# A state-space scan in eight chunks: a ring of eight units, one C product for two units, and the layer norm before it moved into the expert stage

## The chip, the cores and the metric

The kernel runs on one core of a Trainium2 chip. The core has a matrix engine (TensorE, here PE, with its weight loads PEld), three vector engines (VectorE or DVE, ScalarE or ACT, GpSimd or POOL) and SyncE (SP), which here only issues DMAs. Each engine works through its own queue strictly in the order written; the engines meet through semaphores. The metric is the time of one execution on the device in microseconds (us), lower is better.

## The reference, cut to what matters

Two layers of a transformer with adaptive layer norm work on 2048 tokens of 512 features. Layer 0 is a softmax attention and a layer of eight experts (each token goes to one). Layer 1 is a selective state space and an MLP on permuted features. The change touches the end of layer 0 and the state space:

```python
x = x + gb * experts(h)                       # layer 0's end
h = layernorm(x) * (1 + ca) + sa              # the norm before the state space
proj = h @ W_in.T; u, gate = split(proj, 2)   # 1024 channels each
u = silu(causal_conv4(u) + conv_b)
dt, B, C = split(u @ Wx.T, [32, 48])          # each RMS-normalised; B and C have 16 states
delta = softplus(dt @ Wdt.T + dt_bias)
state = exp(delta * A) * state + (delta * u) * B     # for each token, channel and state
y = (state * C).sum(states) + u * D
x = x + ga * ((y * silu(gate)) @ W_out.T)
```

## The kernel before, in words

The program is a row of stages (`qkv`, `attention`, `experts`, `state_space`, `permuted_mlp`), each with its own block of five instruction streams; a stage begins when the one before has ended on all engines. Between stages the activations lie in device memory.

**The end of `experts`.** Tokens are sorted by expert, multiplied tile by tile (23 tiles, L922), scaled on DVE (L1085) and stored. Then POOL gathers the results of the 16 token tiles back (L848), DVE adds each to x (L1089), PE turns it so that features lie on partitions (L931), ACT copies it out (L972) and SP stores it to `x_layer0`, features by tokens (L818).

**The state space.** The 2048 tokens go in 8 chunks of 256 (`SCH`, `SW`), the 1024 channels in 8 tiles of 128 (`DT`). The scan works in units: one unit is four of a tile's 16 states for 128 channels, laid out as 128 partitions (32 channels by 4 states) times 4 groups of channels (`J`) times 256 tokens. A tile has 4 units (`GROUPS`), a chunk 32 (`UNITS`), the whole run 256. For unit q of chunk c:
- SP has stored delta and delta*u of the tile and loaded them back repeated on all state partitions (`repeat`, L1246 to L1256, two slots), and B and C rows as well (`bc_rows`).
- ACT writes the decays exp(delta*A) into PSUM, two instructions of 256 for each half bank, three half banks in all (`decays`, L1636). It waits until the scans that use a half bank have read it.
- The input (delta*u)*B of 1024 elements a partition is written into a place of the ring `scan`, by POOL for even units (L1328) and by DVE for odd ones (L1745, `spread`). The ring has `RING = 4` places; a place is free when PE has summed the unit that used it.
- DVE scans: four instructions of 256 tokens (L1760); after an odd unit it carries the last states over (L1765).
- POOL multiplies the unit by C in place (L1343), one instruction of 1024 elements.
- PE sums over states (L1467, eight instructions), and after the fourth unit adds u*D (L1472). DVE gates the tile into `y` (`gate_y`, L1774), at the unit after next but one: at q = 2 mod 4 it gates the tile before.

All other work of the stage is woven in at fixed units. The table `AT` gives for each unit q of a chunk the product that PE does before it sums unit q: projections, convolution, gates and rows of the next chunk, the layer norm's products of the chunk after that, the output of the chunk before. They share two PSUM banks; each waits until the product two places earlier has been read. `U_COPY`, `CONV_OUT`, `GATE_OUT`, `STEP_OUT` and others give the unit before whose decays ACT reads them; `CENTRED`, `NORM`, `RESIDUAL`, `DELTA` and others the same for DVE. Before the scan, `FIRST` lists chunk 0's products and the layer norm of chunk 1. The layer norm with features on partitions takes a mean and a variance product on PE, a centring (L1700) and a scaling (L1706) of 1024 elements on DVE and squares on ACT. The output (L1457) is multiplied by the gate ga and added to x on DVE (`residual`, L1780).

## Time and profile before

| | us |
|---|---|
| median of 3 runs | 1993.42 |
| lowest, highest | 1985.92, 1998.05 |
| profiled execution, its own time | 1997.48 |
| span of its trace | 1995.7 |

The page of the profile, busy time and share of the span: PE 1644.5 us (82%), PEld 881.9 (44%), DVE 1394.3 (70%), ACT 1083.1 (54%), POOL 998.4 (50%). The mean granted clock of TensorE is 0.818 of full speed. In 40 equal slices, each digit the busy share in tenths:

```profile
PE   6888999999689994869689697896978969755758
PEld 2522232232256443747356474663746637422422
DVE  3258888886173112048999989899899898999523
ACT  2334666667511112265857668576685766754227
POOL 0000000001054004138898888888888888999413
PEclk8766999999855995869588696896978969766778
DMA  5311000000292436233443444434444344544122
```

One slice is 49.9 us. The stages: the attention fills slices 4 to 11, the experts 11 to 16, the state space runs from 784.65 us to about 1897 us (slices 16 to 38), the MLP takes the rest. A row for a group reads: line, engine, operation, written<-read by the program's names, shapes, xcount, then busy us and mean ns of one, then the engine's idle time before it and what released it. PEclk is the clock that the throttle granted, 1.0 being 2.4 GHz and 0.5 being 1.2 GHz.

### The profile page before, as it was taken

To read this page: it belongs to the slowest core of one execution; us is meant where nothing else is said; L and a number is where in the kernel's file an instruction comes from. 1 tells how busy PE (TensorE), PEld (TensorE's weight loads), DVE (VectorE), ACT (ScalarE), POOL (GpSimd) and SP (SyncE) were. 2 spreads that over 40 slices of the span, in tenths; PEclk is the share of its full clock that TensorE was granted. 3 is DMA by queue.
4 is the path that set the end of the run, shared out by engine and by line. 5 is a ranking of instruction groups with operands and counts; after the bars stand their busy time and mean duration, and the time that the engine had idled before them with its cause. 6 is when DMAs were issued, how large, how long until landed. Compare 5 with 4: busy or idle time off the path is not lost. (4 is left out here: it accounts for less than half of the span.)

```text
span 1995.7 us, 24404 instructions
## 1 busy us (share of the span) xinstructions
PE 1644.5 (82%) x8256; PEld 881.9 (44%) x8256; DVE 1394.3 (70%) x2276; ACT 1083.1 (54%) x1989; POOL 998.4 (50%) x590
## 2 busy tenths in 40 slices
PE   6888999999689994869689697896978969755758
PEld 2522232232256443747356474663746637422422
DVE  3258888886173112048999989899899898999523
ACT  2334666667511112265857668576685766754227
POOL 0000000001054004138898888888888888999413
PEclk8766999999855995869588696896978969766778
DMA  5311000000292436233443444434444344544122
GB/s 220 150 55 50 3 3 3 3 3 4 40 354 98 132 111 231 95 89 92 112 101 85 109 119 108 111 80 106 112 114 117 82 102 106 120 102 98 35 100 85
DMA packets 150747, 191.58 MB, mean 96 GB/s; under 512 B 17715, under 2 KB 122947, under 8 KB 148958
## 3 DMA queue, kind: packets, MB, share of 16 engines
q1 hardware_dynamic: 142508, 167.19, 30.9%
...
q8 instruction: 66, 1.08, 0.2%
q14 instruction: 57, 0.47, 0.1%
...
## 5 line engine op out<-in xcount | busy, mean ns | idle before, releaser
L1760 DVE TENSOR_TENSOR_SCAN ssm_scan<-ssm_psum,ssm_state,ssm_scan 128x256 f32<-128x256 f32 x1024 | 678.7, 728 | 49.8 <-ACT ssm_psum L1636 49.3
L1343 POOL TENSOR_TENSOR ssm_scan<-ssm_scan,ssm_bc 128x1024 f32<-128x1024 f32 x256 | 553.5, 2175 | 60.0 <-DVE ssm_scan L1760 58.8
L1636 ACT ACTIVATE ssm_psum<-ssm_rep,ssm_a 128x256 f32<-128x256 f32 x1024 | 433.4, 468 | 168.4 <-DVE ssm_scan L1760 167.9
L1467 PE MATMUL ssm_psum<-ssm_scan,ssm_select 128*32 128x256 f32 x2048 | 204.7, 481 | 199.3 <-POOL ssm_scan L1343 199.2
L1328 POOL TENSOR_TENSOR ssm_scan<-ssm_rep,ssm_bc 128x1024 f32<-128x1024 f32 x128 | 301.1, 2353 | 62.8 <-PE ssm_psum L1467 53.1
L640 ACT ACTIVATE att_probs<-att_psum 128x1024 f32<-128x1024 f32 x256 | 248.3, 1021 | 104.5 <-PE att_psum L576 104.2
L677 DVE TENSOR_REDUCE att_rowmax<-att_psum 128x1 f32<-128x512 f32 x448 | 277.9, 682 | 38.0 <-PE att_psum L558 38.0
L1467 PEld LDWEIGHTS ssm_psum<-ssm_scan,ssm_select 128*32 128x32 f32 x2048 | 45.8, 119 | 316.4 <-POOL ssm_scan L1343 216.4
L529 POOL COPY att_v<-v_tokens 128x128 f32<-128x128 f32 x8 | 2.3, 292 | 328.0 <-ACT att_out L634 328.0
L558 PE MATMUL att_psum<-att_k,att_q 72*128 72x512 bf16 x448 | 159.3, 395 | 3.7 <-DVE att_rowmax L677 2.2
L1745 DVE TENSOR_TENSOR ssm_scan<-ssm_rep,ssm_psum 128x1024 f32<-128x1024 f32 x128 | 155.5, 1215 | 8.5 <-PE ssm_psum L1467 5.8
L1408 PE MATMUL ssm_psum<-ssm_h,ssm_win 128*128 128x256 f32 x512 | 133.0, 419 | 9.6 <-DMA ssm_win<-in_win 6.1
L587 PE MATMUL att_psum<-att_probs,att_v 128*32 128x512 f32 x1024 | 137.2, 608 | 0.6 <-ACT att_probs L640 0.6
L576 PE MATMUL att_psum<-att_q,att_k 74*128 74x512 bf16 x448 | 132.2, 379 | 0.7 <-ACT att_probs L640 0.2
L1457 PE MATMUL ssm_psum<-ssm_y,ssm_wout 128*128 128x256 f32 x512 | 131.9, 417 | 0.6 <-DVE ssm_y L1774 0.6
L1408 PEld LDWEIGHTS ssm_psum<-ssm_h,ssm_win 128*128 128x128 f32 x512 | 108.1, 214 | 33.6 <-issue 15.9
L1416 PE MATMUL ssm_psum<-ssm_upre,ssm_conv 128*128 128x256 f32 x512 | 120.3, 388 | 0.0
L1457 PEld LDWEIGHTS ssm_psum<-ssm_y,ssm_wout 128*128 128x128 f32 x512 | 107.0, 212 | 26.7 <-issue 5.0
L1450 PE MATMUL ssm_psum<-ssm_h,ssm_win 128*128 128x256 f32 x512 | 118.0, 384 | 0.1
L1416 PEld LDWEIGHTS ssm_psum<-ssm_upre,ssm_conv 128*128 128x128 f32 x512 | 95.7, 191 | 24.4 <-issue 11.6
L1450 PEld LDWEIGHTS ssm_psum<-ssm_h,ssm_win 128*128 128x128 f32 x512 | 95.4, 190 | 21.3 <-issue 9.0
L558 PEld LDWEIGHTS att_psum<-att_k,att_q 72*128 72x128 bf16 x448 | 35.1, 98 | 132.0 <-DVE att_rowmax L677 96.1
...
## 6 DMA issues: line engine op xcount, KB each, us to landing
ssm_rep<-drive_rows SPq DMA_DIRECT2D x256, 256.0 KB, 4.4
...
```

The lines of the kernel that those rows point to most:

```text
L558: nc.tensor.matmul(ps_m[n % MB], q[0:QROWS, tile[m // QC]], k[0:QROWS, chunk[m % QC]], start=True, stop=True).then_inc(max_scored, 1)
L640: nc.scalar.activation(probs[:, u % RING, :].rearrange("p (j t) -> p j t", j=2), ps_s[u % 2], ACT.Exp).then_inc(exp_done, 1)
L677: nc.vector.tensor_reduce(rowmax[:, m:m + 1], ps_m[n % MB], AX.X, ALU.max).then_inc(max_done, 1)
L1328: nc.gpsimd.tensor_tensor(drive[:, Q % RING], rep[:, s % 2, 1], bc[:, c % 2, 0, gr, :].unsqueeze(1).to_broadcast([P, J, SW]), ALU.mult).th ...
L1343: nc.gpsimd.tensor_tensor(read[:, Q % RING], drive[:, Q % RING], bc[:, c % 2, 1, gr, :].unsqueeze(1).to_broadcast([P, J, SW]), ALU.mult).t ...
L1408: last = nc.tensor.matmul(halves("proj", c, pair)[:, i], win[:, k, m:m + P], h[:, k, :], start=(k == 0), stop=(k == KT - 1))
L1416: last = nc.tensor.matmul(halves("conv", c, pair)[:, i], conv[:, 2 * pair + i, k, :], upre[:, pair % 2, i, k:k + SW], start=(k == 0), stop ...
L1450: last = nc.tensor.matmul(halves("gate", c, pair)[:, i], win[:, k, m:m + P], h[:, k, :], start=(k == 0), stop=(k == KT - 1))
L1457: last = nc.tensor.matmul(bank("out", c, m)[:, 0:SW], wout[:, t, m * P:(m + 1) * P], y[:, c % 2, t, :], start=(t == 0), stop=(t == DT - 1))
L1467: last = nc.tensor.matmul(ps_y[t % 2][32 * j:32 * j + 32, :], select[:], read[:, Q % RING, j, :], start=(gr == 0), stop=False)
L1636: nc.scalar.activation(ps_decay[n % HALF_BANKS][:, i], rep[:, s % 2, 0, j, :], ACT.Exp, scale=amat[:, t, gr, j:j + 1]).then_inc(decay_done, 1)
L1760: nc.vector.tensor_tensor_scan(drive[:, Q % RING, j, :], ps_decay[(2 * Q + j // 2) % HALF_BANKS][:, j % 2], drive[:, Q % RING, j, :], stat ...
```

## The change

- **Ring.** `RING` goes from 4 to 8 places. To make room the weights of the state space lie in the buffer that held the expert weights, u in a buffer shared with the experts' tail, and `y` is gone: the gated output overwrites its gate. So a new gate may be copied only after the output product that reads the old one; the outputs move from units 16, 17, 27, 28 to 10, 11, 12, 14, the gate products from 10, 11, 12, 14 to 16, 17, 27, 28, and the gate's SiLU from unit 20 to 31.
- **C product.** POOL issues one product of 2048 elements after each odd unit, for it and the even unit before, and its own input for even units three units ahead instead of two.
- **Layer norm.** It is computed in the tail of `experts`, with tokens on partitions: DVE adds, takes statistics, normalises every fourth tile; ACT takes square roots and normalises the others; PE turns the normalised rows, ACT copies them, SP stores x (tokens by features) and the normalised rows (features by tokens). The state space only modulates them. The input half of `W_in` is loaded on ACT's queue in that tail.
- **Output.** `W_out` is multiplied by ga once on POOL; x is added by PE, as products of x's rows against the identity into the same bank (two per output); ACT copies the result out.
- **Chunk 0.** Two of its gate products, two of its step products and the gate's SiLU move behind the start of the scan (units 0 to 5).

```diff
+            pe.wait_ge(y_done, TILES)
             for t in range(TT):
-                pe.wait_ge(x2_done, t + 1)
-                if t >= len(ps_x2):
-                    pe.wait_ge(x2_out, t - len(ps_x2) + 1)
+                pe.wait_ge(*normalised(t))
+                if t >= len(ps_hn):
+                    pe.wait_ge(hn_out, t - len(ps_hn) + 1)
                 for k in range(KT):
-                    last = nc.tensor.transpose(ps_x2[t % len(ps_x2)][:, k * P:(k + 1) * P], x[:, t, k * P:(k + 1) * P], g.ident[:])
-                last.then_inc(x2_mm, 1)
+                    last = nc.tensor.transpose(ps_hn[t % len(ps_hn)][:, k * P:(k + 1) * P], back[:, t, k * P:(k + 1) * P], g.ident[:])
+                last.then_inc(hn_mm, 1)
...
+            act.wait_ge(y_mm, TILES)
+            wsrc = d["win"].rearrange("(k p) m -> p k m", p=P)
+            act.dma_start(win[:, :, 0:DI], wsrc[:, :, 0:DI]).then_inc(g.win_in[0], 16)
+
+            def deviation2(t):
+                act.wait_ge(var2_done, t + 1)
+                nc.scalar.activation(sd[:, t:t + 1], meanvar[:, t, 1:2], ACT.Sqrt, bias=g.ln_eps[:, 0:1]).then_inc(sd2_done, 1)
+
+            def normalise2(t):
+                act.wait_ge(shift2_done, on_act(t) + 1)
+                nc.scalar.activation(back[:, t], x[:, t], ACT.Identity, bias=shift2[:, t:t + 1], scale=rstd[:, t:t + 1]).then_inc(hn_act, 1)
+
+            def turn_out(t):
+                c, at = t // TC, t % TC * P
+                act.wait_ge(hn_mm, t + 1)
+                if c >= TSLOTS and t % TC == 0:
+                    act.wait_ge(g.hn_stored[c % TSLOTS], 16 * (c // TSLOTS))
+                nc.scalar.copy(hnt[:, c % TSLOTS, :, at:at + P], ps_hn[t % len(ps_hn)].rearrange("p (k t) -> p k t", k=KT)).then_inc(hn_out, 1)
+
+            for n in range(TT + 4):
+                if 0 <= n - 1 < TT:
+                    deviation2(n - 1)
+                if 0 <= n - 2 < TT and n - 2 not in DVE_NORMS:
+                    normalise2(n - 2)
+                if n - 4 >= 0:
+                    turn_out(n - 4)
...
+            for n in range(TT + 2):
+                if 0 <= n - 2 < TT:
+                    inverse2(n - 2)
+                if n < TT:
+                    add(n)
+                if 0 <= n - 1 < TT:
+                    variance2(n - 1)
+                if 0 <= n - 2 < TT:
+                    normalise2(n - 2)
+                if n < TT:
+                    statistics2(n)
...
-    RING = 4
+    RING = 8
...
-        AT = {0: ("proj", 0), 1: ("proj", 1), 3: ("conv", 0), 4: ("proj", 2), 5: ("conv", 1), 6: ("proj", 3), 7: ("conv", 2), 8: ("mean", 0),
-              9: ("conv", 3), 10: ("gate", 0), 11: ("gate", 1), 12: ("gate", 2), 13: ("rows", 0), 14: ("gate", 3), 15: ("square", 0),
-              16: ("out", 0), 17: ("out", 1), 18: ("var", 0), 19: ("rms", 0), 20: ("bcast", 0), 21: ("step", 0), 22: ("step", 1),
-              24: ("step", 2), 25: ("step", 3), 27: ("out", 2), 28: ("out", 3)}
-        AHEAD = {"proj": 1, "conv": 1, "gate": 1, "rows": 1, "square": 1, "rms": 1, "step": 1, "mean": 2, "var": 2, "bcast": 2, "out": -1}
-        FIRST = (("mean", 0, 0), ("var", 0, 0), ("bcast", 0, 0), ("proj", 0, 0), ("proj", 0, 1), ("conv", 0, 0), ("proj", 0, 2), ("conv", 0, 1),
-                 ("proj", 0, 3), ("conv", 0, 2), ("conv", 0, 3), ("gate", 0, 0), ("gate", 0, 1), ("rows", 0, 0), ("gate", 0, 2), ("square", 0, 0),
-                 ("gate", 0, 3), ("rms", 0, 0), ("step", 0, 0), ("step", 0, 1), ("step", 0, 2), ("step", 0, 3),
-                 ("mean", 1, 0), ("var", 1, 0), ("bcast", 1, 0))
+        AT = {0: ("proj", 0), 1: ("proj", 1), 3: ("conv", 0), 4: ("proj", 2), 5: ("conv", 1), 6: ("proj", 3), 7: ("conv", 2),
+              9: ("conv", 3), 10: ("out", 0), 11: ("out", 1), 12: ("out", 2), 13: ("rows", 0), 14: ("out", 3), 15: ("square", 0),
+              16: ("gate", 0), 17: ("gate", 1), 19: ("rms", 0), 21: ("step", 0), 22: ("step", 1),
+              24: ("step", 2), 25: ("step", 3), 27: ("gate", 2), 28: ("gate", 3)}
+        AHEAD = {"proj": 1, "conv": 1, "gate": 1, "rows": 1, "square": 1, "rms": 1, "step": 1, "out": -1}
+        FIRST = (("proj", 0, 0), ("proj", 0, 1), ("conv", 0, 0), ("proj", 0, 2), ("conv", 0, 1), ("proj", 0, 3), ("conv", 0, 2), ("conv", 0, 3),
+                 ("rows", 0, 0), ("square", 0, 0), ("rms", 0, 0), ("step", 0, 0), ("gate", 0, 0), ("gate", 0, 1), ("step", 0, 1))
+        LATE = {0: ("gate", 2), 1: ("step", 2), 2: ("gate", 3), 3: ("step", 3)}
...
-        U_COPY, CONV_OUT, GATE_OUT = {3: 0, 4: 1, 7: 2, 9: 3}, {6: 0, 8: 1, 10: 2, 12: 3}, {13: 0, 14: 1, 15: 2, 17: 3}
-        SILU, ROWS_OUT, RMS, SQUARE, GATE_SILU, RSTD, H_OUT = 13, 16, 18, 19, 20, 21, 24
+        U_COPY, CONV_OUT, GATE_OUT = {3: 0, 4: 1, 7: 2, 9: 3}, {6: 0, 8: 1, 10: 2, 12: 3}, {18: 0, 19: 1, 29: 2, 30: 3}
+        SILU, ROWS_OUT, RMS, GATE_SILU, H_OUT = 13, 16, 18, 31, 24
+        LATE_GATE, LATE_STEP, LATE_SILU, LATE_DELTA = {2: 2, 4: 3}, {3: 2, 5: 3}, 5, {3: 2, 5: 3}
...
-        CENTRED, NORMED, NORM = 11, 21, 22
+        NORMED = 21
         DELTA = {24: 0, 25: 1, 27: 2, 28: 3}
-        RESIDUAL = {19: 0, 20: 1, 30: 2, 31: 3}
+        OUT_COPY = {12: 0, 13: 1, 14: 2, 16: 3}
...
+            pool.wait_ge(g.win_in[2], 16)
+            pool.wait_ge(row_out, 1)
+            for t in range(DT):
+                nc.gpsimd.tensor_tensor(wout[:, t], wout[:, t], gate_row, ALU.mult).then_inc(wout_gated, 1)
+
             drive_input(0, 0)
             drive_input(0, 1)
-            for Q in range(2):
+            for Q in range(4):
                 if not ON_DVE[Q]:
                     spread(Q)
             for c in range(SCH):
                 for q in range(UNITS):
                     t, gr = q // GROUPS, q % GROUPS
                     Q = c * UNITS + q
-                    if Q + 2 < SCH * UNITS and not ON_DVE[(q + 2) % UNITS]:
-                        spread(Q + 2)
-                    pool.wait_ge(scan_done, (Q + 1) * J)
-                    nc.gpsimd.tensor_tensor(read[:, Q % RING], drive[:, Q % RING],
-                                            bc[:, c % 2, 1, gr, :].unsqueeze(1).to_broadcast([P, J, SW]), ALU.mult).then_inc(read_done, 1)
+                    if gr % 2:
+                        if Q + 3 < SCH * UNITS:
+                            spread(Q + 3)
+                        pool.wait_ge(scan_done, (Q + 1) * J)
+                        pair = slice((Q - 1) % RING, Q % RING + 1)
+                        nc.gpsimd.tensor_tensor(read[:, pair], drive[:, pair],
+                                                bc[:, c % 2, 1, gr - 1:gr + 1, :].unsqueeze(2).to_broadcast([P, 2, J, SW]), ALU.mult).then_inc(read_done, 2)
...
             def output(c, m):
                 if m == 0:
                     pe.wait_ge(ygate_done, (c + 1) * DT)
+                    pe.wait_ge(wout_gated, DT)
                 for t in range(DT):
-                    last = nc.tensor.matmul(bank("out", c, m)[:, 0:SW], wout[:, t, m * P:(m + 1) * P], y[:, c % 2, t, :], start=(t == 0), stop=(t == DT - 1))
+                    nc.tensor.matmul(bank("out", c, m)[:, 0:SW], wout[:, t, m * P:(m + 1) * P], gate[:, c % 2, t, :], start=(t == 0), stop=False)
+                if m == 0:
+                    pe.wait_ge(xres_in, 16 * (c + 1))
+                for s in range(ST):
+                    last = nc.tensor.matmul(bank("out", c, m)[:, s * P:(s + 1) * P], xres[:, s, m * P:(m + 1) * P], g.ident[:], start=False, stop=(s == ST - 1))
                 last.then_inc(out_mm, 1)
...
-                    act.wait_ge(ygate_done, (c - 1) * DT)
+                    act.wait_ge(out_mm, (c - 1) * KT)
...
+            def copy_out(c, m):
+                act.wait_ge(out_mm, c * KT + m + 1)
+                if m == 0:
+                    act.wait_ge(wout_gated, DT)
+                    if c >= 1:
+                        act.wait_ge(x3_stored, 16 * c)
+                nc.scalar.copy(xout[:, m, :], bank("out", c, m)[:, 0:SW]).then_inc(x3_done, 1)
...
+            modulate(1)
+            copy_rows(0)
+            inverse_rms(0)
+            step_out(0, 0)
             copy_gate(0, 0)
             copy_gate(0, 1)
-            copy_rows(0)
-            copy_gate(0, 2)
-            inverse_rms(0)
-            copy_gate(0, 3)
-            for pair in range(DP):
-                step_out(0, pair)
-            silu_gate(0)
-            norm_chunk(1)
+            step_out(0, 1)
...
-                nc.vector.tensor_tensor(y[:, c % 2, t, :], ps_y[t % 2], gate[:, c % 2, t, :], ALU.mult).then_inc(ygate_done, 1)
-
-            def residual(c, m):
-                if m == 0:
-                    dve.wait_ge(xres_in, 16 * (c + 1))
-                dve.wait_ge(out_mm, c * KT + m + 1)
-                nc.vector.scalar_tensor_tensor(xres[:, m, :], bank("out", c, m)[:, 0:SW], gates[:, m:m + 1], xres[:, m, :],
-                                               ALU.mult, ALU.add).then_inc(x3_done, 1)
...
```

On SP's queue the load of a chunk's rows now waits for that chunk's buffer (two instead of one), `store(c - 1)` stands before the fifth tile of chunk c instead of `store(c - 2)` before the first, and the rows of x for the output are loaded before tile 1 instead of tile 2.

## Rows read from the trace of the kernel before

**Rows 1.** Busy time by stretch: PE, PEld, DVE, ACT, POOL, then clock, DMA.
```profile
1257.74:1383.00 125.26, 106.71 (x596) 70.63 (x596) 113.70 (x186) 84.47 (x188) 110.52 (x56) 0.84 0.44 104
...
1757.00:1872.00 115.00, 57.27 (x344) 24.70 (x344) 109.97 (x175) 55.05 (x126) 110.20 (x55) 0.61 0.37 91
```

**Rows 2.** Waits from 1257 to 1383 us: total, times, longest.
```profile
ACT ssm_upre L1548 <- PE ssm_psum L1408: 11.3, 4, 5.2
...
DVE ssm_scan L1760 <- ACT ssm_psum L1636: 7.5, 6, 2.6
```

**Rows 3.** Timeline of DVE (start, us, instruction): last carry of chunks 0 and 6.
```profile
1007.75 0.17 DVE L1765 TENSOR_REDUCE ssm_state<-ssm_scan 128x8 f32<-128x8 f32 x1
...
1758.59 0.17 DVE L1765 TENSOR_REDUCE ssm_state<-ssm_scan 128x8 f32<-128x8 f32 x1
```

**Rows 4.** Groups by line and shape: busy us, mean ns, idle before.
```profile
L1343 POOL TENSOR_TENSOR ssm_scan<-ssm_scan,ssm_bc 128x1024 f32<-128x1024 f32 x256 | 553.5, 2175 | 60.0 <-DVE ssm_scan L1760 58.8
...
L1328 POOL TENSOR_TENSOR ssm_scan<-ssm_rep,ssm_bc 128x1024 f32<-128x1024 f32 x128 | 301.1, 2353 | 62.8 <-PE ssm_psum L1467 53.1 <-DMA ssm_rep<-drive_rows 9.6
...
L1316 POOL TENSOR_TENSOR ssm_du<-ssm_delta,ssm_u 128x256 f32<-128x256 f32 x64 | 46.6, 728 | 54.5 <-DVE ssm_delta L1734 54.5
...
L1700 DVE TENSOR_TENSOR ssm_x<-ssm_x,ssm_psum 128x1024 f32<-128x1024 f32 x8 | 9.6, 1201 | 20.0 <-PE ssm_psum L1384 20.0
...
L1780 DVE SCALAR_TENSOR_TENSOR ssm_xres<-ssm_psum,mod,ssm_xres 128x256 f32<-128x256 f32 x32 | 15.0, 470 | 17.6 <-PE ssm_psum L1457 17.6
...
L1001 DVE BATCH_NORM_STATS2 moe_stat<-moe_x 128x6 f32<-128x512 f32 x16 | 11.0, 685 | 0.0
```

**Rows 5.** Timelines of POOL, PE and ACT around the same stretch.
```profile
1256.99 4.30 POOL L1343 TENSOR_TENSOR ssm_scan<-ssm_scan,ssm_bc 128x1024 f32<-128x1024 f32 x2
...
1261.35 1.08 PE L1467 MATMUL ssm_psum<-ssm_scan,ssm_select 128*32 128x256 f32 x8 [1.05 <-POOL ssm_scan L1343]
...
1263.38 5.66 PE L1408 MATMUL ssm_psum<-ssm_h,ssm_win 128*128 128x256 f32 x16
...
1269.53 3.72 PE L1408 MATMUL ssm_psum<-ssm_h,ssm_win 128*128 128x256 f32 x16
...
1273.18 0.64 PE L1467 MATMUL ssm_psum<-ssm_scan,ssm_select 128*32 128x256 f32 x8
...
1269.07 0.59 ACT L1548 COPY ssm_upre<-ssm_psum 128x512 f32<-128x512 f32 x1 [5.15 <-PE ssm_psum L1408]
...
1269.55 1.67 ACT L1636 ACTIVATE ssm_psum<-ssm_rep,ssm_a 128x256 f32<-128x256 f32 x4
```

**Rows 6.** Timeline of PE: four single matmul instructions against the identity.
```profile
1215.36 1.06 PE L1398 MATMUL ssm_psum<-ident,ssm_rstd 128*128 128x128 f32 x4
```

**Rows 7.** Timeline of DVE at the start of chunk 3.
```profile
1257.85 1.22 DVE L1745 TENSOR_TENSOR ssm_scan<-ssm_rep,ssm_psum 128x1024 f32<-128x1024 f32 x1
...
1258.99 2.67 DVE L1760 TENSOR_TENSOR_SCAN ssm_scan<-ssm_psum,ssm_state,ssm_scan 128x256 f32<-128x256 f32 x4
...
1264.54 0.42 DVE L1774 TENSOR_TENSOR ssm_y<-ssm_psum,ssm_gate 128x256 f32<-128x256 f32 x1
```

**Rows 8.** Groups by line: SiLU and the table loads around it.
```profile
L1561 ACT ACTIVATE ssm_u<-ssm_u 128x2048 f32<-128x2048 f32 x8 | 15.3, 1910 | 0.1
...
L1518 ACT ACT_TABLE_LOAD x17 | 21.8, 1283 | 4.9 <-PEq L716 4.6
```

**Rows 9.** Timeline of ACT: starts of two successive step outputs, chunk 0.
```profile
857.03 0.84 ACT L1597 ACTIVATE ssm_delta<-ssm_psum,ssm_dtb 128x256 f32<-128x256 f32 x2 [1.75 <-PE ssm_psum L1443]
...
859.86 0.83 ACT L1597 ACTIVATE ssm_delta<-ssm_psum,ssm_dtb 128x256 f32<-128x256 f32 x2
```

**Rows 10.** Timelines of SP, PE and DVE: head of the state space.
```profile
784.65 0.36 SPq L1224 DMA_DIRECT2D ssm_x<-x_layer  x1
...
806.41 8.96 PE L1408 MATMUL ssm_psum<-ssm_h,ssm_win 128*128 128x256 f32 x32 [6.08 <-DMA ssm_win<-in_win]
...
883.66 1.22 DVE L1745 TENSOR_TENSOR ssm_scan<-ssm_rep,ssm_psum 128x1024 f32<-128x1024 f32 x1 [2.69 <-ACT ssm_psum L1623]
```

286 lines of the change are left out of this document (134 added, 152 removed).

## The prediction

> **What bounds the kernel now.** I read the page first: its slices show DVE and POOL full over the last six tenths, the state space, with PE's clock between 0.5 and 0.9 there, and the chain that ended last lies in the last stage and says nothing of the scan. So the busy time by stretch came next: in chunk 3 (126 us) DVE is busy 113.7 us, POOL 110.5, PE 106.7 and ACT 84.5, at a clock of 0.84 [rows 1]. No engine is full; the chunk is longer than any of them, so what matters is who waits in the ring. DVE's largest wait there is for the decays that ACT writes (7.5 us), and ACT is late because it waits in order for PE's products (11.3 us for the inner projection alone) [rows 2]. PE in turn takes its work strictly in order: the product listed for unit q, then the sum over states of unit q, which waits for POOL's C product. From the last carry of chunk 0 to that of chunk 6 six chunks take 1758.59 - 1007.75 = 750.8 us, 125.1 each [rows 3]; this is the number to predict anew. Chunk 0 runs from DVE's first input at 883.7 to 1007.8, 124 us; chunk 7 ends near 1872, 114 us.
>
> **The loads.** POOL: a C product of 1024 elements takes 2.175 us, du of 256 takes 0.728 [rows 4]. The slope is 1.447/768 = 1.88 ns an element and 0.25 us fixed, so one of 2048 takes 4.1 us (upper end: two now, 4.30, from start to end [rows 5]). Saved: 0.2 x 16 = 3 us of POOL per chunk. DVE loses a centring and a normalising of 1.2 each and four residuals of 0.47 [rows 4]: 4.3 us per chunk, to about 110. PE loses the layer norm's products, about 7 us, and gains 16 instructions against the identity in four outputs; four of that kind take 1.06 [rows 6], so an output goes from 3.65 to 4.5. ACT changes by under 1 us, but the gate's SiLU moves to unit 31. With all waits gone a chunk would take DVE's 110 us. That is one end.
>
> **Where the pair sits.** The other end comes from the C product for two units. Its result is ready only after the odd unit's scans, 4.1 us later; PE cannot sum even the even unit before, and the product listed for an odd unit stands in PE's queue behind that sum. Write D for the end of an odd unit's scans. Now the sum of unit q-1 can start 2.2 us after unit q-1; then it starts at D + 4.15, one unit and two microseconds later. But ACT and DVE still want results at the old places, and ACT can't go further ahead: its decays fill three half banks, so it is at most one and a half units in front of DVE, and this is not changed.
>
> I use: scans of a unit 2.62, DVE's input for the next odd unit 1.14 before an even one, gating 0.36 (starts in [rows 7]); the sum 0.57 and a projection 3.65 at full clock, 1.0 and 5.4 at half clock (0.64 and 3.72 against 1.08 and 5.66, less the drain); a copy 0.48 (0.73 for a convolution, an estimate) and the first decays 0.87 before DVE can scan (1.67 for four) [rows 5]. SiLU with its two table loads 1.91 + 2 x 1.28 = 4.5 [rows 8]; a step output 2.83 [rows 9]. Each place then gives a stall:
> - Gating of y at every fourth unit needs the last tile's sum. Where the odd unit has a projection: D + 4.15 + 0.57 + 3.65 + 0.57 + 0.53 = D + 9.5, and DVE is there at D + 6.5: 3.0 us, four times (units 3, 7, 11, 27).
> - An odd unit's product copied three units on: D + 4.15 + 0.57 + 3.65 + 0.48 + 0.87 = D + 9.7 against D + 7.9: 1.8 us, four times (1, 5, 9, 13).
> - Two units on: the second gate product (17, copied at 19) and the third (27 at 29), D + 9.7 against D + 4.2 to 4.8: 5.5 and 4.9, which takes in the stall at 27 above.
> That is 3 x 3.0 + 4 x 1.8 + 10.4 = 27 us, so at least 110 + 27 = 137 a chunk. Then the outputs, now at 10, 11, 12, 14 and copied on ACT one or two units later, queue behind each other on PE at 4.5 each (4.5 + 2 + 6 us more); SiLU at 13 and the root mean square at 21 (about 2.5 each, part of it there today).
>
> Laying all 32 units out in order with these numbers, each start the latest of what it waits for, I get the ends of the odd units 1, 3, ..., 31 at full clock: 6.5, 13.4, 21.4, 30.7, 39.1, 47.2, 62.8, 69.7, 82.7, 95.0, 103.4, 110.3, 120.0, 127.5, 139.8, **150.6**. With the half clock's durations for the work that follows wherever PE has stood for a C product, I lay it out again: 6.5, 16.5, 23.3, 35.3, 43.8, 51.9, 69.3, 76.2, 91.0, 105.5, 114.7, 121.6, 132.6, 140.1, 154.6, **165.5**. POOL has about 109 us of work in either and only follows; the ring's eight places are never full; the repeated rows, in SP's queue behind the store and the loads that move, land before their input is due in both.
>
> The trace decides between the two clocks: after PE has stood for C products at a chunk's start the first projection takes 5.66 us, 1.2 GHz for most of it, where the next takes 3.72 at 2.4 [rows 5]; with PE busy in 84% of a chunk the clock is granted at 0.84, in 50% at 0.61 [rows 1]. In the new chunk PE is busy about 101/160 = 63%, nearer the second. I take 160. The Trainium skill speaks to both sides of this. "TensorE: Matmul & The Clock Gate", section "What's actually happening", says that for a model the ramp's penalty is under 1% of a typical span; by that the chunk would be 150.6. Its section "HAM oscillation" says that a loop in which the engine waits in every round pays the ramp in every round; the rows above agree with this one.
>
> **The sum.** Chunks 1 to 6: 6 x (160 - 125.1) = +209. Chunk 0 has the same and two step outputs, a gate's SiLU and a gate copy besides, 2 x 2.83 + 4.5 + 3.65, about 13: 160 + 13 - 124 = +49. Chunk 7 has only the outputs: DVE's 105, some 12 of stalls, 117 against 114: +3. The end: a product of 4.1 for 2.2, a second sum, four outputs longer by about 1: +7. The head, from 784.65 to the first input on DVE at 883.66 [rows 10]: the layer norm before the first projection goes (21.8 us become 7, a load and a modulation), chunk 1's goes (about 15), two step outputs and SiLU go into chunk 0 (10), but the repeated rows then set the start (9 back), and the experts' tail is longer. There DVE adds (0.69), takes statistics (0.685 [rows 4]), three small ones near 0.16 and a normalising share: 1.9 a tile for 16 tiles where the gathers bring one in 1.4, about 8, of which 4 reach the next stage. I take -27 (ends -36 and -10). The input half of the weights is loaded in that tail and costs nothing there; without that cover it would be at most 8 us. The gating of the output weights on POOL (8 x 1.3) lies before its first du; if late, 5. Storing the residual rows turned the other way: between 0 and 3.
>
> Sum: 209 + 49 + 3 + 7 - 27 = +241. On the profiled execution's 1997.5 that is 2238; the median of before is 4 below it, so **2235**.
>
> **The rivals.** (a) The ring unhooks the engines. Place: POOL's input for an even unit, which waits today for PE's sum of four units ago (53 us over the run [rows 4]); with eight places that is gone, and if PE's and ACT's lateness is only carried and not created, a chunk falls to DVE's 110 plus 2. Then 6 x -13, chunk 0 about +1, chunk 7 -6, end +5, head -27: -105, **1888**. It decides if an odd unit's product were done within D + 5.1, i.e. if PE did not have to wait for the pair; the program's order speaks against it. Chance 0.07. (b) Only the first three kinds of stall show and PE's queueing hides in them: 137 to 142 a chunk, 6 x 14 + 28 + 3 + 7 - 27, **2090**. For it: layouts by hand tend to add waits that overlap. Chance 0.13. (c) The layout holds and PE keeps 2.4 GHz: 150.6, 6 x 25.5 + 40 + 3 + 7 - 27 = +176, **2170**; chance 0.2. (d) It holds, with half clock wherever PE stood: 165.5, +280, **2273**; with my forecast between them, chance 0.52 for both. (e) The gains and losses meet within 1%: 0.03. (f) Beyond 2300, by waits that I have not seen such as the repeated rows': 0.05.
>
> **How the numbers follow.** The forecast is the case between (c) and (d). (b) to (d) hold 0.85 and span 2090 to about 2290; I cut the lower edge of (b): 2090 to 2300. The likeliest case's own range is 2200 to 2290. A change of under 1% can't be told from none here. Faster 0.07, same 0.03, slower 0.90.
>
> **What would show it.** Right: chunks of 150 to 165 us; PE's wait for the C product (L1343's successor) becoming its largest, in the early part of a chunk too; DVE's wait for decays growing from 7.5 to over 30 us a chunk, most at units 12, 13, 16, 19, 29; POOL busy under 75% of a chunk; PE's clock in the scan below 0.8. Wrong: chunks near 112 with DVE over 95% busy (rival a), or a head that isn't shorter. It is wrong altogether if PE's sum of an even unit starts before the odd unit's scans end.

## The result

The changed kernel takes **2306.1 us** (median of five, 2297.1 to 2310.1) where the kernel before takes 1993.4 beside it: ratio **1.156, 95% interval 1.151 to 1.162**, slower. The forecast was 2235 with a range to 2300, so the direction and the place were right and the size was too small by 71 us. Of that 44 us lie in chunks 1 to 6 and 17 in the last chunk; the profiled execution shows 59 of the 71, since it is 9 us below its kernel's median where that of before is 4 above.

The profiled execution took 2297.1 us, with a span of 2295.3. Busy time by stretch comes first: chunks 1, 2, 6 and 7, then from the last carry to the end. The columns are the length of the stretch, PE, PEld, DVE, ACT, POOL with their numbers of instructions, the granted clock, the DMA share and GB/s.

```profile
1030.50:1198.00 167.50, 113.49 (x584) 73.44 (x584) 111.50 (x182) 84.95 (x190) 109.17 (x40) 0.76 0.34 79
1198.00:1368.20 170.20, 115.52 (x584) 75.35 (x584) 111.49 (x182) 85.00 (x191) 109.18 (x40) 0.77 0.34 78
...
1869.80:2034.30 164.50, 109.16 (x584) 70.87 (x584) 111.58 (x182) 82.96 (x187) 109.20 (x40) 0.79 0.34 77
2034.30:2167.60 133.30, 55.17 (x352) 28.89 (x352) 106.98 (x168) 54.69 (x129) 102.82 (x36) 0.60 0.34 77
2167.60:2295.30 127.70, 89.13 (x486) 42.31 (x486) 31.36 (x32) 51.88 (x79) 24.82 (x25) 0.82 0.20 75
```

Against [rows 1] DVE has 2 us less to do in a chunk and POOL 1.4 less, and the chunk is 42 us longer: nothing new is computed there, the engines stand. POOL is busy in 109.2 of 167.5 us, 65%. So the second view is who waits, in chunk 1 (total, times, longest):

```profile
PE ssm_psum L1535 <- POOL ssm_scan L1431: 53.9, 11, 8.8
POOL ssm_scan L1431 <- DVE ssm_scan L1808: 42.9, 12, 7.8
DVE ssm_scan L1808 <- ACT ssm_psum L1695: 40.4, 12, 8.9
...
ACT ssm_gate L1662 <- PE ssm_psum L1513: 19.1, 4, 8.2
ACT late_turned L1608 <- PE ssm_psum L1479: 15.6, 4, 6.3
POOL ssm_scan L1409 <- DMA ssm_rep<-drive_rows: 15.5, 8, 3.8
...
ACT ssm_upre L1599 <- PE ssm_psum L1469: 12.5, 4, 6.4
ACT ssm_xout L1675 <- PE ssm_psum L1525: 9.2, 3, 4.0
```

The first three lines are one ring, and the ACT lines say where it closes. PE waits for the C product, POOL for the scans of the odd unit, DVE for the decays, and ACT, which writes the decays, for products that PE has not begun because it stands in the first line. DVE waited 7.5 us for decays in a chunk before [rows 2]; now it is 40.4. Over the whole run, groups by line (busy us, mean ns, then the idle time before them):

```profile
L1808 DVE TENSOR_TENSOR_SCAN ssm_scan<-ssm_psum,ssm_state,ssm_scan 128x256 f32<-128x256 f32 x1024 | 678.6, 729 | 299.7 <-ACT ssm_psum L1695 298.3
L1431 POOL TENSOR_TENSOR ssm_scan<-ssm_scan,ssm_bc 128x2048 f32<-128x2048 f32 x128 | 532.5, 4160 | 311.0 <-DVE ssm_scan L1808 311.0
...
L1535 PE MATMUL ssm_psum<-ssm_scan,ssm_select 128*32 128x256 f32 x2048 | 217.9, 524 | 483.6 <-POOL ssm_scan L1431 483.0
```

The C product of two units takes 4160 ns, as worked out; twice the single one was 4350 [rows 4]. It saves 21 us of POOL's time over the run, on an engine that is not the bound.

The ring can be watched at the start of chunk 1, in the timelines of POOL, PE and ACT (start, us, instruction, the idle time before it):

```profile
1030.59 4.16 POOL L1431 TENSOR_TENSOR ssm_scan<-ssm_scan,ssm_bc 128x2048 f32<-128x2048 f32 x1 [3.70 <-DVE ssm_scan L1808]
...
1034.80 1.94 PE L1535 MATMUL ssm_psum<-ssm_scan,ssm_select 128*32 128x256 f32 x16 [8.83 <-POOL ssm_scan L1431]
...
1037.68 5.29 PE L1469 MATMUL ssm_psum<-ssm_h,late_weights 128*128 128x256 f32 x16
...
1043.48 3.72 PE L1469 MATMUL ssm_psum<-ssm_h,late_weights 128*128 128x256 f32 x16
...
1043.01 0.59 ACT L1599 COPY ssm_upre<-ssm_psum 128x512 f32<-128x512 f32 x1 [6.37 <-PE ssm_psum L1469]
1043.49 1.67 ACT L1695 ACTIVATE ssm_psum<-ssm_rep,ssm_a 128x256 f32<-128x256 f32 x4
```

PE stands 8.8 us for the product of units 30 and 31, sums both (1.94 us at the low clock), and only then starts the projection that ACT has to copy before it may write the next decays. ACT stands 6.4 us in front of it. The projection takes 5.29 us after the wait and 3.72 a unit later, as in [rows 5].

### The profile page after: what moved, and what is told of

The parts are those of the page before. It is cut to its first block and busy times, and to the rows that moved or that the text cites. A ratio compares the mean times of both kernels' runs of the same rounds, so it can differ in the third digit from the quotient of the medians.

```text
span 2295.3 us, 24260 instructions
## 1 busy us (share of the span) xinstructions
PE 1668.3 (73%) x8168; PEld 896.0 (39%) x8168; DVE 1383.9 (60%) x2292; ACT 1094.1 (48%) x2026; POOL 991.8 (43%) x470
## 3 DMA queue, kind: packets, MB, share of 16 engines
q8 instruction: 65, 1.06, 0.2%
## 5 line engine op out<-in xcount | busy, mean ns | idle before, releaser
L1431 POOL TENSOR_TENSOR ssm_scan<-ssm_scan,ssm_bc 128x2048 f32<-128x2048 f32 x128 | 532.5, 4160 | 311.0 <-DVE ssm_scan L1808 311.0
L1535 PE MATMUL ssm_psum<-ssm_scan,ssm_select 128*32 128x256 f32 x2048 | 217.9, 524 | 483.6 <-POOL ssm_scan L1431 483.0
L1535 PEld LDWEIGHTS ssm_psum<-ssm_scan,ssm_select 128*32 128x32 f32 x2048 | 56.0, 130 | 592.2 <-issue 335.5
L1513 PE MATMUL ssm_psum<-ssm_h,late_weights 128*128 128x256 f32 x512 | 144.5, 446 | 0.0
L1479 PE MATMUL ssm_psum<-ssm_upre,late_weights 128*128 128x256 f32 x512 | 134.4, 421 | 0.0
L1469 PE MATMUL ssm_psum<-ssm_h,late_weights 128*128 128x256 f32 x512 | 127.4, 406 | 7.2 <-ACT ssm_h L1590 7.1
L1513 PEld LDWEIGHTS ssm_psum<-ssm_h,late_weights 128*128 128x128 f32 x512 | 115.5, 230 | 32.4 <-issue 12.5
L1521 PE MATMUL ssm_psum<-ssm_gate,late_weights 128*128 128x256 f32 x512 | 122.3, 393 | 0.6 <-issue 0.6
L1479 PEld LDWEIGHTS ssm_psum<-ssm_upre,late_weights 128*128 128x128 f32 x512 | 106.1, 212 | 31.6 <-issue 15.0
L1469 PEld LDWEIGHTS ssm_psum<-ssm_h,late_weights 128*128 128x128 f32 x512 | 104.2, 206 | 29.9 <-issue 13.4
L1521 PEld LDWEIGHTS ssm_psum<-ssm_gate,late_weights 128*128 128x128 f32 x512 | 98.3, 196 | 23.8 <-issue 10.3
L1662 ACT COPY ssm_gate<-ssm_psum 128x512 f32<-128x512 f32 x32 | 18.7, 585 | 148.3 <-PE ssm_psum L1513 148.3
```

What stands on the lines that cost most here:

```text
L1431: nc.gpsimd.tensor_tensor(read[:, pair], drive[:, pair], bc[:, c % 2, 1, gr - 1:gr + 1, :].unsqueeze(2).to_broadcast([P, 2, J, SW]), ALU.m ...
L1469: last = nc.tensor.matmul(halves("proj", c, pair)[:, i], win[:, k, m:m + P], h[:, c % 2, k, :], start=(k == 0), stop=(k == KT - 1))
L1479: last = nc.tensor.matmul(halves("conv", c, pair)[:, i], conv[:, 2 * pair + i, k, :], upre[:, pair % 2, i, k:k + SW], start=(k == 0), stop ...
L1513: last = nc.tensor.matmul(halves("gate", c, pair)[:, i], win[:, k, m:m + P], h[:, c % 2, k, :], start=(k == 0), stop=(k == KT - 1))
L1521: nc.tensor.matmul(bank("out", c, m)[:, 0:SW], wout[:, t, m * P:(m + 1) * P], gate[:, c % 2, t, :], start=(t == 0), stop=False)
L1535: last = nc.tensor.matmul(ps_y[t % 2][32 * j:32 * j + 32, :], select[:], read[:, Q % RING, j, :], start=(gr == 0), stop=False)
```

## The experiments

Ratios are to the kernel before on the same chip, where it took 1987.7 to 1995.5 us; so a difference of a few us between the times of two rows can be that of two chips. "Chunk" is the mean over chunks 1 to 6 between last carries (125.1 us before, 167.3 after); chunk 7 is 113.5 before and 133.3 after; both are read from the one profiled execution of each kernel. Diffs are against the changed kernel unless another is named.

| kernel | us | ratio (95%) | chunk | chunk 7 |
|---|---|---|---|---|
| single C products | 2025.1 | 1.015 (1.011 to 1.020) | 132.0 | 113.1 |
| the same, ring of four | 2031.3 | 1.018 (1.012 to 1.025) | 132.8 | 112.9 |
| pair, products before sums | 2100.6 | 1.052 (1.047 to 1.057) | 140.2 | 131.7 |
| pair, dt*x first | 2289.4 | 1.146 (1.142 to 1.151) | 168.3 | 123.5 |
| pair, filler on PE | 2252.4 | 1.131 (1.125 to 1.137) | 161.4 | 130.2 |
| before, even sum waits for odd unit | 2081.3 | 1.041 (1.037 to 1.047) | 135.8 | 130.2 |
| norm's move alone | 1977.9 | 0.993 (0.991 to 0.996) | 124.3 | 115.4 |
| single, later copies | 1984.2 | 0.995 (0.993 to 0.997) | 126.1 | 110.0 |
| pair with all three repairs | 1996.7 | 1.001 (0.998 to 1.004) | 126.4 | 118.1 |
| norm's move, dt*x first | 1967.8 | 0.986 (0.981 to 0.992) | 123.2 | 115.6 |
| pair, later copies alone | 2182.7 | 1.098 (1.092 to 1.104) | 149.7 | 129.4 |
| single, later copies, dt*x first | 1985.1 | 0.995 (0.992 to 0.998) | 125.7 | 111.7 |

**1. Single C products.** The whole change but the pair; POOL's own input goes back to two units ahead with it:

```
-                    if gr % 2:
-                        if Q + 3 < SCH * UNITS:
-                            spread(Q + 3)
-                        pool.wait_ge(scan_done, (Q + 1) * J)
-                        pair = slice((Q - 1) % RING, Q % RING + 1)
...
+                    if Q + 2 < SCH * UNITS and not ON_DVE[(q + 2) % UNITS]:
+                        spread(Q + 2)
+                    pool.wait_ge(scan_done, (Q + 1) * J)
+                    nc.gpsimd.tensor_tensor(read[:, Q % RING], drive[:, Q % RING],
+                                            bc[:, c % 2, 1, gr, :].unsqueeze(1).to_broadcast([P, J, SW]), ALU.mult).then_inc(read_done, 1)
```

> The changed kernel with one C product of 1024 elements for each unit again, all else as changed (ring of eight, outputs at 10, 11, 12, 14, gates at 16, 17, 27, 28, SiLU of the gate at 31, layer norm in the experts' tail). Theory (the pair product puts each odd unit's PE product one unit and two microseconds later, and ACT and DVE wait for it): the stalls at units 6, 8, 19, 29 go, chunks of 118 to 128 us for 167, time 1930 to 1990 us. Rival (the moved outputs, gates and SiLU make the stalls): chunks stay above 150, time above 2150.

2025.1 us: 281 of the 313 us are gone with the pair, and more than expected stays, 1.5% above the kernel before. Chunks 1 to 6 are 7 us each above the 125.1 of before, and the carries show where: in chunk 1 the step from unit 11 to 13 takes 12.6 us (43.6 to 56.2 after the chunk's start), before 9.2; that from 27 to 31 takes 22.2 (110.2 to 132.5), before 14.7. There stand the copies of the outputs and the gate, whose places the change moved.

**2. The same with a ring of four** (`RING = 8` becomes 4).

> The changed kernel with single C products and the ring back at four places; places, layer norm and output as changed. It says with the ring of eight what the ring alone is worth. Theory (POOL's input waits for PE's sum of four units ago, 53 us over the run before): 10 to 40 us above the same kernel with eight places, 1960 to 2010 us. Rival (PE's own work sets the pace in the early part of a chunk, so the ring is worth nothing): within 5 us of it.

1.018 against 1.015, and the intervals overlap: the rival held, the eight places by themselves give nothing that this measurement shows. POOL's input did wait for PE's sum before [rows 4], but without it a chunk is under 1 us shorter. Four places were not tried with the pair, nor with the later copies of experiment 8.

**3. The pair's wait alone, in the kernel before.** The even unit's sum waits for the odd unit's product too; POOL still computes single products:

```
-                pe.wait_ge(read_done, Q + 1)
+                pe.wait_ge(read_done, Q + 1 + (Q + 1) % 2)
```

> The kernel before with one wait changed: PE's sum of an even unit waits for the C product of the odd unit after it too. Products stay single, the ring four, all places as before. Theory (latency of the pair in PE's order): gating needs D + 2.2 + 0.57 + 3.65 + 0.57 + 0.53 = D + 7.5 against D + 6.5, and POOL's inputs, two units ahead in a ring of four, wait for sums that come a unit later: 8 to 25 us a chunk more, time 2060 to 2190 us. Rival (PE has slack to take the wait; the loss lies in the rest of the change): 1985 to 2010 us.

2081.3 us, 4% slower with no other change. The wait of PE, without the double product, costs 10.7 us a chunk and 16.7 in chunk 7. It is not the 42 us that the changed kernel lost, so the wait needs something else beside it. The double product with the outputs and gates at their old places was not run, so how the 42 us divide between the product's own length and the moved places is not shown. With four places in the ring POOL is held as well: its input waits 21.1 us for PE's sum in chunk 2, where it waited 53 in the whole run before [rows 4]. From the waits of that chunk in this kernel:

```profile
PE ssm_psum L1467 <- POOL ssm_scan L1343: 27.1, 9, 6.5
POOL ssm_scan L1328 <- PE ssm_psum L1467: 21.1, 16, 3.1
```

**4. The pair, PE's products before both sums.** The products listed for an even and an odd unit are issued ahead of the two sums, so that none stands behind the wait:

```
-                for q in range(UNITS):
-                    for key in at(c, q):
+                for q in range(0, UNITS, 2):
+                    for key in at(c, q) + at(c, q + 1):
                         misc(*key)
                     sum_states(c, q)
+                    sum_states(c, q + 1)
```

> The changed kernel, pair product kept; only PE's order within a pair of units differs: the products listed for the even and the odd unit both come before the two sums, which wait for the pair product. Theory (what costs is that the odd unit's product stands behind a sum that waits for the pair): gating needs D + 4.15 + 2 x 0.57 + 0.53 = D + 5.8 and is met at D + 6.5, the copies at 19 and 29 find their products, stalls remain only where PE is full (outputs); chunks 122 to 135, time 1980 to 2070 us. Rival (the pair product's own 4.1 us in the loop is what costs, wherever the product stands): less than 10 us a chunk gained, time above 2240.

2100.6 us, above what was expected by 30: the order gives back 205 of 313 us, and the chunk falls from 167.3 to 140.2 with the double product as it was. ACT's waits in chunk 2 of this kernel, beside DVE's for the decays and POOL's for the repeated rows:

```profile
DVE ssm_scan L1809 <- ACT ssm_psum L1696: 24.5, 11, 7.4
...
POOL ssm_scan L1409 <- DMA ssm_rep<-drive_rows: 20.0, 8, 3.9
ACT ssm_xout L1676 <- PE ssm_psum L1525: 15.9, 3, 9.7
```

The largest of ACT's waits that are left stands at the outputs' copies, up to 9.7 us at one of them. That is one of the two places of experiment 1.

**5. The pair, dt*x ahead of the C product on POOL**, at the unit where both are due:

```
+                    c2, t2 = ahead(c, t)
+                    if c2 < SCH and gr == DRIVE:
+                        drive_input(c2, t2)
                     if gr % 2:
                         pool.wait_ge(scan_done, (Q + 1) * J)
...
-                    c2, t2 = ahead(c, t)
-                    if c2 < SCH and gr == DRIVE:
-                        drive_input(c2, t2)
```

> The changed kernel with du of the tile two ahead issued on POOL before the pair's C product and not after it. Theory: in chunk 7, which has no other work, POOL waits for the repeated rows (19.7 us there) because du now follows a product of 4.16 us that itself starts one unit later, and the gating waits behind it; chunk 7 falls from 133 us to 112 to 120 and the other chunks by 0 to 3 each: time 2265 to 2290 us. Rival (chunk 7 is long by the outputs' copies alone): no change, 2295 to 2310.

Chunks 1 to 6 do not change (168.3); chunk 7 goes from 133.3 to 123.5 us, less than the 112 to 120 that were expected. POOL in chunk 7 of the changed kernel shows why:

```profile
2041.60 4.15 POOL L1431 TENSOR_TENSOR ssm_scan<-ssm_scan,ssm_bc 128x2048 f32<-128x2048 f32 x1
2045.71 0.72 POOL L1397 TENSOR_TENSOR ssm_du<-ssm_delta,late_turned 128x256 f32<-128x256 f32 x1
...
2055.82 2.35 POOL L1409 TENSOR_TENSOR ssm_scan<-ssm_rep,ssm_bc 128x1024 f32<-128x1024 f32 x1 [2.95 <-DMA ssm_rep<-drive_rows]
```

dt*x, from which the repeated rows are made, stands behind a product of 4.15 us, and POOL's input for a later unit then waits for their transfer: 19.7 us in the chunk, by this row of its waits.

```profile
POOL ssm_scan L1409 <- DMA ssm_rep<-drive_rows: 19.7, 7, 4.3
```

With the order turned, the same row of chunk 7 reads:

```profile
POOL ssm_scan L1409 <- DMA ssm_rep<-drive_rows: 1.9, 4, 0.6
```

In chunks 1 to 6 POOL waits for rows too (15.5 us in chunk 1, above, and 3.2 with the order turned), but the chunks' length does not depend on it. The other 10 us of chunk 7 are not the rows': PE still waits 70.8 us for the C product there, and in experiment 3 the wait for the pair alone made chunk 7 16.7 us longer.

**6. A filler on PE.** At eleven units of a chunk, before the wait for the C product, 16 narrow matmuls with weights of zero (32 instructions in the trace) are added into the sum's accumulation:

```
+                fill = c >= 1 and q in FILL
+                if fill:
+                    for n in range(16):
+                        j = n % 4
+                        nc.tensor.matmul(ps_y[t % 2][32 * j:32 * j + 32, :], zero[:], skip[:, 0:2, :], start=(gr == 0 and n < 4), stop=False)
                 pe.wait_ge(read_done, Q + 1)
```

> The changed kernel with filler on PE: before the sums of units 2, 8, 12, 16, 18, 20, ..., 30 of chunks 1 to 7, 32 instructions of zero weights are added into the tile's open sum (about 2.3 us at 2.4 GHz, 4 at 1.2), where PE stands for the pair product. Theory (half clock after such waits costs what lies between the two layouts, 150.6 and 165.5 us a chunk): if the granted clock rises to 0.9, 5 to 12 us less a chunk, time 2220 to 2270 us. Rival (the order of the waits costs the same at either clock, or the filler is in the way): 2295 to 2350 us.

2252.4 us, 54 less than the changed kernel, though PE does more. The two profiled executions are 45 us apart: 38 of it lie in chunks 1 to 7, where the filler stands, and 6 ahead of the scan, where the two kernels do the same work. The mean granted clock goes from 0.792 to 0.840. In chunk 2 of this kernel:

```profile
1186.70:1348.00 161.30, 128.77 (x936) 81.52 (x936) 111.00 (x181) 84.44 (x189) 109.34 (x40) 0.85 0.35 81
```

and from its timeline of PE, after the wait at the chunk's start:

```profile
1193.88 4.70 PE L1472 MATMUL ssm_psum<-ssm_h,late_weights 128*128 128x256 f32 x16
```

The clock in the chunk is 0.85 where it was 0.77, and the projection takes 4.70 us where the one after the same wait took 5.16 in chunk 2 of the changed kernel. It is not 3.72 yet. If the filler acts by the clock alone, which no run separates, 38 us is a lower bound of what the low clock costs here, 1.7% of the run. It is still far from the pair's 281.

**7. The norm's move alone.** Single products, ring of four, the products' and copies' old places and a separate buffer for y; what stays of the change is the layer norm in the experts' tail with its loads, its transposed residual and the output weights that carry the gate. Besides the edits of 1 and 2:

```
-              9: ("conv", 3), 10: ("out", 0), 11: ("out", 1), 12: ("out", 2), 13: ("rows", 0), 14: ("out", 3), 15: ("square", 0),
-              16: ("gate", 0), 17: ("gate", 1), 19: ("rms", 0), 21: ("step", 0), 22: ("step", 1),
-              24: ("step", 2), 25: ("step", 3), 27: ("gate", 2), 28: ("gate", 3)}
+              9: ("conv", 3), 10: ("gate", 0), 11: ("gate", 1), 12: ("gate", 2), 13: ("rows", 0), 14: ("gate", 3), 15: ("square", 0),
+              16: ("out", 0), 17: ("out", 1), 19: ("rms", 0), 21: ("step", 0), 22: ("step", 1),
+              24: ("step", 2), 25: ("step", 3), 27: ("out", 2), 28: ("out", 3)}
...
-                nc.vector.tensor_tensor(gate[:, c % 2, t, :], ps_y[t % 2], gate[:, c % 2, t, :], ALU.mult).then_inc(ygate_done, 1)
+                nc.vector.tensor_tensor(y[:, c % 2, t, :], ps_y[t % 2], gate[:, c % 2, t, :], ALU.mult).then_inc(ygate_done, 1)
```

> The layer norm in the experts' tail, the weights' early load, the output with x added on PE and the shortened head alone: ring of four, single C products, the buffer y back, outputs at 16, 17, 27, 28 and gates at 10, 11, 12, 14 with SiLU at 20 as before. Theory: head 29 us shorter, chunk 0 some 12 longer, DVE 4.3 and PE 6 us less a chunk of which a half to all shows: 1940 to 1970 us. Rival (DVE and PE waits take that work's place): only the head's gain, 1975 to 1985 us.

1977.9 us, 0.993: this part is a gain, of 10 to 13 us (by the medians on its chip and by the ratio), in the rival's range and above the theory's. By the last carries 12.0 us are won by the end of chunk 0 (995.8 against 1007.8), 5.3 in chunks 1 to 6, and 1.9 and 3.1 are lost in chunk 7 and at the end. The 12.0 understate the move: the first addition of the experts' tail, ahead of which the kernels do the same work, starts at 758.0 us in this execution and at 750.9 in that of before. Over all profiled executions it starts between 739.8 and 758.2, so times counted from the start of a trace are uncertain by that much; the lengths of chunks do not carry it.

**8. Single products, later copies.** Experiment 1 with the copies one unit further from their products:

```
-        U_COPY, CONV_OUT, GATE_OUT = {3: 0, 4: 1, 7: 2, 9: 3}, {6: 0, 8: 1, 10: 2, 12: 3}, {18: 0, 19: 1, 29: 2, 30: 3}
+        U_COPY, CONV_OUT, GATE_OUT = {3: 0, 4: 1, 7: 2, 9: 3}, {6: 0, 8: 1, 10: 2, 12: 3}, {19: 0, 20: 1, 30: 2, 31: 3}
...
-        OUT_COPY = {12: 0, 13: 1, 14: 2, 16: 3}
+        OUT_COPY = {13: 0, 14: 1, 15: 2, 17: 3}
```

> The ring of eight with single C products (2025 us), but the output products' copies one unit later (13, 14, 15, 17) and the gate products' copies too (19, 20, 30, 31). Theory 1: what is left of the loss without the pair, some 30 us, is ScalarE standing in front of products that TensorE has not finished (50 us on the gate products, 36 us on the outputs in 500 us of it); copied a unit later the waits go and the time is 1975 to 2005 us, the steps from unit 11 to 13 and from 27 to 31 shrink to their former size. Rival: the order on TensorE and the SiLU at unit 31 make the loss, wherever the copies stand; then 2015 us or more.

1984.2 us: the first theory held for the time. The 30 us by which experiment 1 was slower than before are gone with these places, and 10 more. In chunk 2 the step from unit 11 to 13 is 8.4 us (44.0 to 52.4), below the 9.2 of before. The step from 27 to 31 did not shrink to its former size, as the theory had it: it is 19.5 us there, against 22.3 in experiment 1 and 14.7 before. The gate's SiLU with its two table loads stands in it now, at unit 31 (4.5 us on ACT); moving that back alone was not tried. Over the whole run ACT's wait in front of the gate products and DVE's for the decays, in experiment 1 and then here:

```profile
L1660 ACT COPY ssm_gate<-ssm_psum 128x512 f32<-128x512 f32 x32 | 18.8, 586 | 98.8 <-PE ssm_psum L1511 98.8
...
L1806 DVE TENSOR_TENSOR_SCAN ssm_scan<-ssm_psum,ssm_state,ssm_scan 128x256 f32<-128x256 f32 x1024 | 677.7, 729 | 136.8 <-ACT ssm_psum L1693 135.1 <-POOL ssm_scan L1409 1.2
```

```profile
L1660 ACT COPY ssm_gate<-ssm_psum 128x512 f32<-128x512 f32 x32 | 18.7, 585 | 68.7 <-PE ssm_psum L1511 68.7
...
L1806 DVE TENSOR_TENSOR_SCAN ssm_scan<-ssm_psum,ssm_state,ssm_scan 128x256 f32<-128x256 f32 x1024 | 677.9, 729 | 90.8 <-ACT ssm_psum L1693 89.0 <-POOL ssm_scan L1409 1.2
```

30 us less in the first, 46 in the second; the run is 41 shorter by its median, and the profiled executions of these rows are 50 apart.

**9. The pair with three repairs:** products before sums, dt*x first, later copies (the edits of 4, 5 and 8 together).

> The changed kernel with its pair kept and three repairs together: both units' products into PSUM before both sums, dt*x ahead of the C product on GpSimd, and the copies one unit later. Theory 1: the losses lie one behind another and each repair takes its own off: from 2101 us with the products first, some 8 in the last chunk and 25 to 30 at the copies, so 2020 to 2065 us, still above the kernel before, since what the odd unit's product waits for stays. Rival: the pair's wait of TensorE alone sets the time and the copies only stand in it; then 2090 us or more.

1996.7 us, below the range of the first theory and equal to the kernel before. Chunk 2 of this kernel, with double products and all:

```profile
1125.00:1251.40 126.40, 100.00 (x584) 70.58 (x584) 110.89 (x181) 84.74 (x190) 109.30 (x40) 0.82 0.45 105
```

and its waits there:

```profile
PE ssm_psum L1536 <- POOL ssm_scan L1435: 26.5, 9, 9.9
...
POOL ssm_scan L1435 <- DVE ssm_scan L1810: 13.6, 10, 4.7
...
DVE ssm_scan L1810 <- ACT ssm_psum L1697: 11.3, 7, 4.3
```

PE still stands up to 9.9 us for the pair, and the chunk is 126.4 us long, 1.3 more than before: what ACT copies next has been issued ahead of that wait. DVE's 11.3 us of waiting for decays (7.5 before) use up what it saves in work. Both theories were wrong on this point: I had the pair's wait as a loss that stays. On the same chip the kernel with single products and later copies (experiment 8) is 12 us faster (ratios 0.995 and 1.001, intervals apart); in the profiled executions chunk 7 is 8 of that (110.0 against 118.1). The two differ in PE's and POOL's order too, so the 12 us are what the mended pair falls short of that kernel by, not the price of the product alone.

**10. The pair, later copies alone** (the edit of 8, with the pair and both orders as changed).

> The changed kernel with only the copies one unit later (13, 14, 15, 17 and 19, 20, 30, 31), its pair and the order of TensorE and GpSimd as they are. All repairs together gave 1997 us, TensorE's order alone 2101. Theory 1: the time is lost where ScalarE stands in front of a product that TensorE has not begun, since TensorE is held at the first sum by the double C product; with a unit more of distance most of this goes even in the old order: 2050 to 2150 us. Rival: the old order on TensorE makes each product late by a C product whatever the place of its copy, and the remaining copies (of the convolution, of the steps) carry the wait on: 2200 us or more.

2182.7 us: 123 less, but above what the first theory expected by 33 and 17 below the rival's bound. The order on PE gives 205 by itself, the places 123, dt*x 17; that sums to 345, and all three together gave 309. So the repairs add up with little overlap, and the order on PE is the largest. With the old order ACT still waits for the convolution's products, 124.4 us over the run, as the changed kernel does (118.5); with products first it is 29.8. From this kernel:

```profile
L1608 ACT ACTIVATE late_turned<-ssm_psum,ssm_convb 128x256 f32<-128x256 f32 x64 | 26.8, 469 | 124.4 <-PE ssm_psum L1479 124.4
```

and from experiment 4:

```profile
L1609 ACT ACTIVATE late_turned<-ssm_psum,ssm_convb 128x256 f32<-128x256 f32 x64 | 26.7, 467 | 29.8 <-PE ssm_psum L1479 29.8
```

That is the rival's mechanism: the copies that were not moved carry the wait on.

**11. The norm's move, dt*x first** (experiment 7 with the order of 5).

> The kernel with only the layer norm's move (1978 us), with dt*x ahead of the C product on GpSimd at the unit where both are due. Theory 1: in the last chunk TensorE and VectorE wait for the scan's input at the front, and the input's product comes one C product (2 us) earlier: up to 8 us off chunk 7, none off the other chunks, so 1965 to 1978 us. Rival: the repeated rows' transfer ends last there, and the order on GpSimd changes nothing: 1975 to 1982 us with chunk 7 at 115.

1967.8 us, 0.986, the fastest of all and faster than both kernels. The time is in the expected range, but the place was not the expected one: chunk 7 is as long as without it (115.6 and 115.4), chunks 1 to 6 are 1.1 us shorter each. Its interval (0.981 to 0.992) just overlaps that of experiment 7 (0.991 to 0.996), and the two were not measured side by side, so the gain over the kernel before is shown and that of the order alone is not.

**12. Single products, later copies, dt*x first.**

> The ring of eight with single C products and later copies (1984 us), with dt*x ahead of the C product on GpSimd too. Theory 1: the order on GpSimd is worth what it gave to the kernel with the norm's move alone, 10 us in all, so 1970 to 1980 us. Rival: chunk 7 has no wait left here (110 us), and nothing changes: 1981 to 1988 us.

1985.1 us, the same as without dt*x first (1984.2). The rival held: with single products nothing waits there.

## Why the prediction was right in its direction and too small

The terms, each against the profiled executions (own times 1997.5 and 2297.1, spans 1995.7 and 2295.3):

| term | predicted | measured |
|---|---|---|
| chunks 1 to 6 | +209 | 1003.8 - 750.8 = +253 |
| chunk 0 | +49 | 175.6 - 124.1 = +51.5 |
| chunk 7 | +3 | 133.3 - 113.5 = +19.8 |
| end | +7 | 127.7 - 123.6 = +4 |
| head | -27 | 69.9 - 99.0 = -29 |
| sum | +241 | +299.6 |

- **The mechanism held.** PE's sum of an even unit starts after the odd unit's scans, a product for an odd unit stands behind it, ACT in front of that product, and DVE waits for the decays: 40.4 us a chunk where over 30 was named, POOL 65% busy where under 75% was, the clock 0.76 to 0.79 where under 0.8 was. Experiments 1 and 4 showed it: take away either the pair or what stands behind its wait, and 281 or 205 us come back.
- **The layout by hand held nearly; the choice between its two versions failed.** For the low clock's durations the odd units were to end at 6.5, 16.5, 23.3, 35.3, 43.8, 51.9, 69.3, 76.2, 91.0, 105.5, 114.7, 121.6, 132.6, 140.1, 154.6 and 165.5 us. In chunk 1 they end at 6.6, 16.7, 23.6, 35.7, 44.2, 52.3, 69.4, 76.3, 91.7, 106.2, 115.8, 122.6, 134.2, 141.6, 156.7 and 167.5. The failed step is "I take 160": it lies between 150.6 and 165.5, and no mechanism gives a value between them; the measured chunk is 167.3, and six chunks make 44 us of the miss. The choice was made by the clock, and the row on which it rested had 5.66 us for a projection after a wait [rows 5]; in chunk 1 the products of that size that follow a wait take 4.66 to 5.47 us, and 3.62 to 3.72 without one. Two of them:

```profile
1080.09 4.66 PE L1479 MATMUL ssm_psum<-ssm_upre,late_weights 128*128 128x256 f32 x16
...
1177.43 5.47 PE L1513 MATMUL ssm_psum<-ssm_h,late_weights 128*128 128x256 f32 x16
```

  The layout had 5.4 for each, so that it still ends 1.8 us before the measured chunk (11 us in six chunks) is partly luck: other waits take up the time that these products did not, and no run says which. With 165.5 the forecast would have been rival (d), 2273. The case that came is (f), beyond 2300 by waits such as the repeated rows', given 0.05: of the 33 us that 2306 lies above (d), 11 are in chunks 1 to 6 and 17 in chunk 7, where that wait was.
- **The clock.** A rule stood behind the lower version: "TensorE: Matmul & The Clock Gate" of the Trainium skill, section "What's actually happening", puts the ramp's penalty under 1% of a span for a model. Here the filler brought 38 us in the chunks that have it, 1.7%, so the trace disagrees for this kernel if that gain is the clock's; with the page's section "HAM oscillation", on a loop that waits in each round, it agrees.
- **Chunk 7, the second failed step, failed at a sentence without a number:** "the repeated rows ... land before their input is due in both". There is 19.7 us of waiting for them in that chunk, and 9.8 of the 19.8 us that it grew by went when dt*x was moved ahead (experiment 5). The other 10 stand with PE's wait for the pair, which by itself cost 16.7 us there in the kernel before (experiment 3) where the term had "some 12 of stalls"; with all repairs 118.1 is left (experiment 9). The reason for the rows' lateness was in the working already, one product of 4.1 us in front of a 0.73 us instruction on POOL, whose result makes a round trip through two transfers.
- **Rival (a)** said that the ring of eight unhooks the engines if PE does not have to wait for the pair. PE still waits in experiment 9, and the loss is gone all the same: the condition was not the wait but what is queued behind it. The gain of (a), chunks near 112, came in no kernel. With eight places the shortest have 125.7, and DVE is busy 111 of a chunk of 126.4 in experiment 8; eight places in place of four changed nothing that can be measured (experiment 2). That DVE's and ACT's waits of the rest are held up by the three half banks of decays was not tried.
- **Chunk 0** came out right by luck in part: it is 8.3 us longer than a chunk of the middle where 13 were added, and the middle chunk is 7.3 longer than the 160 taken.
- **The head** came out near, by luck in part. The load of the state space's first chunk is issued at 785.00 us and before at 784.65 [rows 10], but this execution was 1.7 us ahead when the experts' tail began: from the tail's first addition on DVE to that load it is 35.9 us (749.11 to 785.00) against 33.8 (750.85 to 784.65). So the tail costs 2.1 us and not 4, and the way from the load to DVE's first input is 69.9 us, not 68.
- **The outputs' four extra instructions** were taken at 0.85 us; 1.06 for four [rows 6] is a low-clock duration. In chunk 1 of the changed kernel they have a row of their own:

```profile
1088.81 0.61 PE L1525 MATMUL ssm_psum<-ident,ssm_xres 128*128 128x128 f32 x4
```

  The sum after them starts at 1089.35, so they add 0.54 us. The end came 3 us shorter than predicted.
